# Second layer norm of a two-layer graph network: its row arithmetic moves from VectorE to GpSimd

## The reference

```python
h = jnp.maximum(_layernorm(x, axis=-1), 0.0)
x = x + _L0_gnn_ref(h, adj, ...)      # convolution, distances and messages, GRU gates
h = jnp.maximum(_layernorm(x, axis=-1), 0.0)   # the second layer norm
x = x + relu(h @ W[:d] + (adj @ h) @ W[d:] + bias)
```

## Time and profile before

| what | value |
|---|---|
| median of 3 runs | 1807.4 us (1806.64 to 1809.37) |
| the profiled execution's own time | 1806.16 us |
| its span, first to last instruction | 1804.4 us |
| PE busy | 1729.2 us (96%) |
| DVE busy | 1475.5 us (82%) |
| ACT busy | 884.0 us (49%) |
| POOL busy | 594.4 us (33%) |
| PE clock granted, mean | 0.994 of full speed |

### The profile page before, as it was taken

One profiled execution on the slowest core, in us unless ns is written; L12 is line 12 of the kernel. 1 busy time (PEld: TensorE's weight loads), 2 busy tenths in 40 slices (PEclk: granted clock), 3 DMA queues, 4 the chain that ended last, 5 costly groups with the idle time before them and its releaser, 6 DMA issues. The chain is left out here.

```text
span 1804.4 us, 36601 instructions
## 1 busy us (share of the span) xinstructions
PE 1729.2 (96%) x12221; PEld 1139.9 (63%) x12222; DVE 1475.5 (82%) x3194; ACT 884.0 (49%) x1617; POOL 594.4 (33%) x744
## 2 busy tenths in 40 slices
PE   3779999999998999999999999999999999999997
PEld 2467777764445666666666666666666666666664
DVE  6789888862346988888888888888888888888886
ACT  4665666665344444444444444444444444444442
POOL 5688777711012222222222222222222222222221
PEclk9899999999999999999999999999999999999999
DMA  6287888769743334334334334334334334334331
GB/s 241 77 302 262 290 304 281 256 230 340 258 141 121 96 100 116 94 100 116 94 100 116 94 101 115 94 101 115 94 102 115 93 104 115 92 105 115 92 107 33
DMA packets 242827, 262.70 MB, mean 146 GB/s; under 512 B 82392, under 2 KB 178639, under 8 KB 242255
## 3 DMA queue, kind: packets, MB, share of 16 engines
q1 hardware_dynamic: 242766, 261.94, 46.1%
HBM read 154.92 MB, written 90.18 MB: 136 GB/s over the span
## 5 line engine op out<-in xcount | busy, mean ns | idle before, releaser
L1568 PE MATMUL ps_rz<-big 128*128 128x512 f16 x2304 | 560.1, 379 | 0.8 <-DVE big L1561 0.8
L1568 PEld LDWEIGHTS ps_rz<-big 128*128 128x128 f16 x2304 | 221.9, 98 | 203.0 <-DVE big L1561 1.0
L1568 PE MATMUL ps_n<-big 128*128 128x256 f16 x2304 | 314.2, 273 | 0.2
L1568 PEld LDWEIGHTS ps_n<-big 128*128 128x128 f16 x2304 | 225.1, 98 | 95.2 <-DVE big L1705 1.2
L1568 PE MATMUL ps_l<-big 128*128 128x512 f16 (+1 forms) x1536 | 272.0, 327 | 8.8 <-DVE big L1807 4.5
L1279 PE MATMUL m_ps<-big 128*128 128x512 f16 (+1 forms) x1152 | 268.3, 375 | 3.2 <-DVE big L1046 2.4
L1736 POOL TENSOR_TENSOR big<-big 128x256 f32<-128x256 f32 x128 | 97.6, 763 | 450.7 <-ACT big L1729 450.7
L1568 PEld LDWEIGHTS ps_l<-big 128*128 128x128 f16 x1536 | 149.9, 98 | 97.2 <-DVE big L1807 5.5
L1568 PE MATMUL ps_b<-big 128*128 128x256 f16 x1536 | 189.9, 273 | 2.1 <-DVE big L1636 2.1
L1711 ACT ACTIVATE big<-big,w_scale 128x512 f32<-128x512 f32 x128 | 92.6, 724 | 177.0 <-DVE big L1702 177.0
L1279 PEld LDWEIGHTS m_ps<-big 128*128 128x128 f16 x1152 | 111.9, 98 | 105.3 <-issue 2.4
(11 more groups left out here) (240 smaller groups left out, 2802.9 us busy)
## 6 DMA issues: line engine op xcount, KB each, us to landing
spectra<-ysb SPq DMA_DIRECT2D x96, 256.0 KB, 3.7
big<-spectra SPq DMA_DIRECT2D x64, 384.0 KB, 3.4
xin<-in_x SPq DMA_DIRECT2D x64, 256.0 KB, 3.4
x_normed<-front SPq DMA_DIRECT2D x64, 256.0 KB, 2.3
h_turned<-front SPq DMA_DIRECT2D x64, 256.0 KB, 3.9
big<-h_turned SPq DMA_DIRECT2D x64, 256.0 KB, 2.7
big<-in_adj SPq DMA_DIRECT2D x64, 256.0 KB, 3.4
big<-in_x SPq DMA_DIRECT2D x64, 256.0 KB, 2.8
```

Of the source, the lines that this page charges most:

```text
L1568: last = pe.matmul(dest, stationary(dl), moving(wl), start=start and n == 0, stop=stop and n == 2, **kw)
```

## The change

The two instructions of `norm2` are issued on POOL, right behind `norm2_rstd`, in place of DVE. POOL makes one more small addition ahead of them into a new tile that nobody reads. The reader that `norm2` waits for is now `h2_low`. DVE waits for `h2hat_done` of the graph before in `x1_stats`, so that it doesn't overwrite the mean that POOL still reads.

```diff
+        rstd_seen = sb("rstd_seen", [P, H])
@@ x1_stats
             ready(dve, "stats2", t, i + 1, H)
+            before(dve, "h2hat_done", t)
             dve.memset(wait_taker[:, 1 + i:2 + i], 0.0)
             dve.bn_aggr(meanvar_b[:, i, :], stats_b[:, i, :]).then_inc(S["aggr2"], 1)
@@ norm2
-        def norm2(dve, t, p):
-            ready(dve, "rstd2", t)
-            before(dve, "h2_high", t)
+        def norm2(pool, t, p):
+            ready(pool, "rstd2", t)
+            before(pool, "h2_low", t)
+            pool.tensor_tensor(rstd_seen[:, :], eps[:, :], eps[:, :], ALU.add)
             for i in range(H):
-                last = dve.tensor_scalar(h2hat[:, i, :], x1[:, p, i, :], meanvar_b[:, i, 0:1], rstd_b[:, i:i + 1],
-                                         ALU.subtract, ALU.mult)
+                last = pool.tensor_scalar(h2hat[:, i, :], x1[:, p, i, :], meanvar_b[:, i, 0:1], rstd_b[:, i:i + 1],
+                                          ALU.subtract, ALU.mult)
             last.then_inc(S["h2hat_done"], 1)
@@ gpsimd slot
                     if prev:
                         norm2_rstd(pool, t - 1, 1 - p)
+                        norm2(pool, t - 1, 1 - p)
@@ vector slot
                         weighted_low(dve, t, p)
-                    if prev:
-                        norm2(dve, t - 1, 1 - p)
```

## The result

The changed kernel takes 1860.96 us (median of 4, 1860.21 to 1861.8) where the kernel before takes 1807.66 us: 53.3 us more, ratio 1.0295 (1.0282 to 1.0308). The prediction was 1857.5, inside a range of 1839 to 1879.

The account below looks back on a forecast made before the run. PE, full in the gates stage, bounds the kernel; a 20.02 us loop replaces its slot: 45.8 us over 61 slots, with the ends +50.3, so 1856.5 profiled, 1857.5 median. Range 1839 to 1879.

Parts of the forecast that it names:

- What bounds, and that nothing can be gained: Gates stage: PE busy 1189.89 of 1190 us sets the 19.28 us slot; removing 0.73 us of DVE work is worth 0.
- The chain on POOL: From L1757: pair of rows 2.43 us, rstd_seen 0.27, rows end at 4.05, L1776 starts at 4.08, 0.74 us later.
- A loop, not a line: Aggregation, POOL, norm2, ACT, DVE's list, next aggregation: once around takes 20.02 us, which becomes the period; slack doesn't help.
- PE's slack: Steady slots, PE's overwrite of ps_n behind DVE's L1705: 0.34 us to spare.
- doesn't add up: Rival: each slot costs PE only the delay over its slack, 0.34 us times 62, giving 1829 us; chance 0.04.
- the 0.91 us before L1658: DVE idle time behind L1757, on a side branch; claimed to give nothing back against the delay.
- The size of a slot: Steady gates slot: 19.28 + 0.74 = 20.02 us, PE standing still 0.74 us in front of ps_n.
- Which way the shift takes: Behind L1776, POOL's conv_add and DVE's list through L1593 to gate_new (L1719) all move by 0.74 us.
- L1593: DVE instruction of 1.62 us beside POOL's L1548; forecast: stall stays; rival: it shrinks, up to 0.27 us a slot; chance 0.09.
- That end of my range: Low end from the rival of a smaller L1593 stall: 16.5 us less, 1841, with 2 us more below.
- The waits and DMAs at 0: h2_low wait, DVE's h2hat_done wait before aggregation, and later pair rows and transpose: each 0; no DMA added.

Follow-up runs that it names:

- the run with one DVE instruction: Kernel before with only half 0 of norm2's rows made by DVE, half 1 keeping a constant: 1807.06 us, ratio 0.9998.
- the pads: Unread small POOL additions: kernel before, ahead of L1761, ten 1826.9 us, five 1808.58 us; kernel after, four ahead of norm2's rows, 1896.55 us.
- the last run above: Kernel after with DVE's L1594 issued ahead of the next slot's h2 split and SP's adjacency load behind the loads of h and x: 1821.79 us.
- the first run with the split in the hole: Kernel after with DVE's adjacency split L1594 issued ahead of the next slot's h2 split, SP's load order unchanged: 1856.42 us.

## Why the prediction was right

- *What bounds, and that nothing can be gained.* Right, and the run with one DVE instruction shows it.
- *The chain on POOL.* The pair took 2.42 us and the small addition 0.18 to its successor (I took 2.43 and 0.27): rows' end at 3.92 in place of 4.05, ACT's split, 0.11 us behind it where I took 0.03, at 4.03 for 4.08. The Trainium skill's rule (GPSIMD Engine Reference, section 4.1 "Engine selection") that one-input operations are roughly line-rate is not borne out: all 128 of the new instructions took 1218 to 1237 ns, three times DVE's 0.41.
- *A loop, not a line.* Right, which is the mechanism that made the number. Shown by the pads: five additions, hidden by what stands beside them, cost about 1 us; ten, by which the norm comes 0.25 us later, less than PE's slack, cost 19.6; behind the threshold 0.59 us a slot cost 35.6. The rival "doesn't add up" falls. My statement that the 0.91 us before L1658 don't help holds too: they shrank to 0.42 and PE waits all the same.
- *The size of a slot.* 20.07 us for 20.02. The term that was mis-sized is the shift of the loop: it was 0.70 up to L1720 (1168.55 - 1159.77 = 8.78 us behind the aggregation, before 8.08) where I had 0.74, and 0.08 came behind it, from L1746, that I had nowhere. The sum is 0.78 by the rows of one slot and 0.80 by the mean of 61 slots, which makes 48.5 us where I had 45.8. The two errors have opposite signs, and that the slot is off by only 0.05 owes something to that. Slot 1 (2.0), slot 63 (0.8 for 0.7) and slot 64 (1.7 for 1.8) came as forecast.
- *Which way the shift takes.* I moved all that is queued behind L1776 by 0.74. `conv_add` in fact started only 0.58 us later (L1545 at 5.75 us behind the aggregation, for 5.17), but this addition took 1.33 us for 1.21, so the next one, L1549, came 0.69 later all the same; why it took longer was not tried. DVE's L1706 came 0.64 later. L1594 ends 0.55 us after L1549, before 0.54, so what carries the shift on to L1720 is POOL's `conv_add` and not DVE's own list.
- *Left out of the sum.* 1.05 us at the very end, with PE at a lower clock, and 0.7 ahead of slot 1. Neither is shown to come from the change (below for the first).
- *Luck.* For the profiled execution I had 1856.5 us, and it took 1861.08, 4.6 more. I then added 1.2 us for the median, but the median lies 0.1 below the profiled execution, so 1.3 us of the miss are hidden. Of the 4.6, 2.7 lie in the 61 slots; 0.7 and 1.0 are the two stretches just named.
- *L1593.* It didn't shrink: 1.68 us, before 1.62. In slot 1 it started ahead of POOL's L1549 again (584.72 and 585.11), as before. That end of my range had no part in the outcome. Its place in the loop is shown by the last run above.
- *The waits and DMAs at 0.* No wait of PE for h2's transpose shows in the steady slots, nor one of DVE before L1758 and L1759.

## What to carry to other kernels

Where one engine sets the slot, as PE did here, relief for another is worth nothing, and a move is priced by the latency it adds between two hand-overs, not by busy time: here 2.42 us for 0.73 on the one chain that goes round. Look for the loop through all engines from one slot to the next; slack inside it is a threshold, behind which each tenth of a microsecond costs 6 us in 62 slots. If an engine of longer latency must do the work, split it so that only what truly depends on the last input stands behind it, and when an instruction is moved, follow every queue that waits for it.

## What the runs showed of the hardware

- POOL's two-input additions held DVE's instructions with two SBUF inputs (L1594 1.68 us beside L1549, 0.74 alone; in the last run L1722 1.14 us beside L1551, 0.43 alone), but POOL's TENSOR_SCALAR with one tensor input didn't: L1720 and L1723 stayed at 0.43 us beside it, and in the first run with the split in the hole L1594 took 0.74 us while L1772 ran to 1161.29. Whether that holds for other shapes wasn't tried. DVE's timeline of that run:

```profile
1160.59 0.74 DVE L1594 SCALAR_TENSOR_TENSOR big<-big,w_scale 128x512 f16<-128x512 f32 x1
```

- Tiles 8 bytes further on made POOL's 128x256 float32 addition 0.09 us longer (852 and 758 ns). Which of its tiles does it was not tried.
- PE's clock at the end: in the kernel after PE idled 4.71 us before the last layer's matmuls (before: 4.26), and the twelve took 5.30 us in place of 4.25. The busy times of that stretch, kernel after and kernel before, show the granted clock (the last column but two) at 0.55 and 0.76, 0.5 being the lower level of 1.2 GHz:

```profile
1845.00:1853.00 8.00, 5.30 (x12) 1.64 (x12) 0.17 (x1) 0.67 (x2) 0.00 (x0) 0.55 0.27 66
```
```profile
1792.00:1799.00 7.00, 4.25 (x12) 1.47 (x12) 0.88 (x2) 0.84 (x2) 0.00 (x0) 0.76 0.21 57
```

The longer wait is not shown to be the reason. In the run with five additions PE waited the 4.26 us of the kernel before, and the twelve took 5.30 us:

```profile
1795.61 5.30 PE L1569 MATMUL ps_l<-big 128*128 128x512 f16 x12 [4.26 <-DMA big<-big]
```

In the kernel after with four more additions the wait was 6.56 us and they took 4.63; over all traces they take between 4.22 and 5.30 us, in no order that the wait explains. So the 1.05 us are not shown to be a price of the change; what set the clock in each trace stays open. The steady waits of 0.6 us a slot left the clock at 1.00.
